# Flamingo block on one core: a re-ordered first stage, opening and border, and TensorE products on zeros

## What is computed

```
x += tanh(g0) * autocorrelation(layernorm(x), ctx, ctx)
x += tanh(g1) * mixture(layernorm(x))          # base product + 8 routed low-rank experts, top 2
x += tanh(g2) * attention(layernorm(x), ctx)   # 32 query heads, 8 key/value heads of 128, RMS norm
x += tanh(g3) * ffn(layernorm(x))              # W plus 8 low-rank updates
```

## Time and profile before

| | us |
|---|---|
| median of 3 runs | 821.94 (816.72 to 822.92) |
| the profiled execution | 821.45 |
| its span, first to last instruction | 819.7 |
| TensorE busy | 782.6 (95%) |
| VectorE busy | 559.7 (68%) |
| ScalarE busy | 415.0 (51%) |
| GpSimd busy | 365.5 (45%) |

### The profile page before, as it was taken

One profiled execution on the slowest core, in us unless ns is written; L12 is line 12 of the kernel. 1 busy time (PEld: TensorE's weight loads), 2 busy tenths in 40 slices (PEclk: granted clock), 3 DMA queues, 4 the chain that ended last, 5 costly groups with the idle time before them and its releaser, 6 DMA issues.

```text
span 819.7 us, 13174 instructions
## 1 busy us (share of the span) xinstructions
PE 782.6 (95%) x4224; PEld 634.8 (77%) x4224; DVE 559.7 (68%) x1235; ACT 415.0 (51%) x1158; POOL 365.5 (45%) x428
## 2 busy tenths in 40 slices
PE   4798889988999999999999999999999999999998
PEld 2354446567888888888888888888888888888776
DVE  4676667755777666777666777666777766777774
ACT  4355545355555644555554556544555554454421
POOL 2356665656333632453354336424632643254532
PEclk9899999998999999999999999999999999999999
DMA  8200001302100300030021002000300111000002
GB/s 302 93 27 27 26 27 34 109 1 90 28 14 1 104 26 1 1 104 27 1 61 57 14 1 91 29 12 1 103 27 1 34 46 52 2 14 1 1 27 77
DMA packets 17123, 34.61 MB, mean 42 GB/s; under 512 B 2336, under 2 KB 2592, under 8 KB 16800
## 3 DMA queue, kind: packets, MB, share of 16 engines
q1 hardware_dynamic: 17056, 33.78, 12.7%
HBM read 31.67 MB, written 2.10 MB: 41 GB/s over the span
## 4 chain that ended last, share of the span: by engine, by line
PE 74%; POOL 8%; DVE 7%; issue 6%; ACT 3%; DMA 1%; SPq 1%; POOLq 0%; ACTq 0%; DVEq 0%
PE pair L837 17%; PE pair L838 17%; PE pair L839 17%; PE pair L936 4%; PE pair L949 3%; PE pair L998 3%; PE pair L850 2%; POOL qkr L515 2%; POOL probn L507 2%; PE pair L938 1%; PE pair L874 1%; PE pair L891 1%; DMA bb<-in_bb 1%; POOL wo_lo L501 1%; PE pair L878 1%
## 5 line engine op out<-in xcount | busy, mean ns | idle before, releaser
L507 POOL TENSOR_TENSOR probn<-prob,erec 128x512 f32<-128x512 f32 x64 | 66.8, 1044 | 162.1 <-DVE erec L1315 162.1
L1320 DVE TENSOR_REDUCE qkss<-qksq 128x5 f32<-128x640 f32 x64 | 52.6, 821 | 90.3 <-ACT qksq L704 90.3
L1339 DVE TENSOR_TENSOR qkn<-pair,qkr 128x640 f32<-128x640 f32 x64 | 52.7, 824 | 89.5 <-POOL qkr L515 89.5
L697 ACT ACTIVATE prob<-score,nmax 128x128 f32<-128x128 f32 x256 | 99.6, 393 | 20.4 <-DVE nmax L1302 18.7
L837 PE MATMUL pair<-wq_hi,nT_hi 128*128 128x512 f32 x256 | 107.4, 420 | 0.0
L686 ACT ACTIVATE oT_hi<-pair 128x512 fp32r<-128x512 f32 x64 | 38.1, 595 | 136.2 <-PE pair L839 136.2
L837 PE MATMUL pair<-wo_hi,oT_hi 128*128 128x512 f32 x256 | 100.8, 394 | 2.8 <-issue 2.8
L839 PE MATMUL pair<-wq_hi,nT_lo 128*128 128x512 f32 x256 | 101.4, 396 | 0.0
L838 PE MATMUL pair<-wq_lo,nT_hi 128*128 128x512 f32 x256 | 101.4, 396 | 0.0
L838 PE MATMUL pair<-wo_lo,oT_hi 128*128 128x512 f32 x256 | 100.3, 392 | 0.0
L839 PE MATMUL pair<-wo_hi,oT_lo 128*128 128x512 f32 x256 | 99.7, 389 | 0.0
(11 more groups left out here) (173 smaller groups left out, 1990.3 us busy)
## 6 DMA issues: line engine op xcount, KB each, us to landing
wq_raw<-in_wq SPq DMA_DIRECT2D x32, 256.0 KB, 3.0
wo_raw<-in_wo SPq DMA_DIRECT2D x32, 256.0 KB, 2.9
wkv_raw<-in_wkv SPq DMA_DIRECT2D x8, 512.0 KB, 4.8
ctxn<-in_ctx_n SPq DMA_DIRECT2D x8, 256.0 KB, 3.1
ctxt<-in_ctx_t SPq DMA_DIRECT2D x8, 256.0 KB, 2.7
out<-wkv_raw SPq DMA_DIRECT2D x8, 256.0 KB, 2.0
xres<-in_x SPq DMA_DIRECT2D x1, 1280.0 KB, 11.0
wbase<-in_wbase SPq DMA_DIRECT2D x1, 1024.0 KB, 8.2
```

Of the source, the lines that this page charges most:

```text
L507: pool.tensor_tensor(probn[:], prob[:], erec[:].unsqueeze(2).broadcast_to([P, HG, P]), ALU.mult).then_inc(normed, 1)
L697: t = act.activation(prob[:, h, :], score[:, h, :], ACT.Exp, bias=nmax[:, h:h + 1], accum_out=esum[:, h:h + 1])
L1320: dve.tensor_reduce(qkss[:], qksq[:], AX.X, ALU.add).then_inc(qk_ss, 1)
L1339: dve.tensor_tensor(qkn[:], qk_bank, qkr[:].unsqueeze(2).broadcast_to([P, HG + 1, P]), ALU.mult).then_inc(qk_nat, 1)
```

## The change

The same instructions run in another order on all engines, with these additions: TensorE multiplies a 128x128 block of zeros (prod1, written by GpSimd as its first instruction) by itself ten times (`WARM`) while the first transfers run, and the identity by itself eight times after `q_transform(1)`; their results are not read. `q_transform(1)` writes the bank base_bank in place of corr_bank. The identity copy and the gating of bb move behind the first pick (`constants`); SP loads context 2 ahead of x of batches 3 to 7, and context 3 ahead of the turned context 1. In a slot, the low parts of weights and turned context precede `lag_weights` on GpSimd, and `low_rows` follows `h_scale`; on ScalarE `high_rows` goes from the end of a slot to the start of the next, and `high_turned_ctx` and `lag_exponents` are done for batch b+1 at the end of slot b. On TensorE `turn_out` goes ahead of the third context transform. At the border, `base_products` of batches 6 and 7 are split in halves, and the last steps of batch 7 go into slots 1 and 2. n1T and spare change places in SBUF.

The diff, with one line of context:

```diff
@@ -95,3 +95,3 @@
     kfb = early("kfb", [P, 4, D])
-    rest8, rest9, spare, wlag = (early(n, [P, CH, P]) for n in ("rest8", "rest9", "spare", "wlag"))
+    rest8, rest9, n1T, wlag = (early(n, [P, CH, P]) for n in ("rest8", "rest9", "n1T", "wlag"))
     op = [early(f"op{i}", [P, D]) for i in range(4)]
@@ -102,3 +102,3 @@
     ctxn = early("ctxn", [P, 2, D])
-    n1, n1T = early("n1", [P, D]), early("n1T", [P, CH, P])
+    n1, spare = early("n1", [P, D]), early("spare", [P, D])
 wo_raw = sb("wo_raw", [P, HG, D])
@@ -195,2 +195,5 @@
 
+def q_spectrum(b):
+    return base_bank if b == 1 else corr_bank
+
 def n2_bank(b):
@@ -215,2 +218,3 @@
 consts = sem("a_consts")
+zeros = sem("a_zeros")
 tanhed = sem("a_gates_tanh")
@@ -318,2 +322,3 @@
 PICK = 4
+WARM = 10
 ROUTE = 6
@@ -381,5 +386,6 @@
         sp.dma_start(bcat[:], bcat_d[:]).then_inc(ld_w[2], 16)
+        load_ctx(2)
         load_batches(2)
+        load_ctx(3)
         load_turned_ctx(1)
-        load_ctx(2)
         sp.dma_start(wkv_raw[:], wkv_d[0]).then_inc(ld_wkv, 16)
@@ -391,4 +397,5 @@
         for b in range(3, B):
+            if b > 3:
+                load_ctx(b)
             load_turned_ctx(b - 1)
-            load_ctx(b)
         load_turned_ctx(B - 1)
@@ -426,2 +433,3 @@
     def _(pool):
+        pool.memset(prod1[:, 0:P], 0.0).then_inc(zeros, 1)
         pool.memset(neghalf[:], -0.5).then_inc(consts, 1)
@@ -465,2 +473,4 @@
         def add_bias(b):
+            if b == 0:
+                pool.wait_ge(bias_gated, 1)
             pool.wait_ge(h_norm, b + 1)
@@ -500,2 +510,3 @@
                 pool.wait_ge(w_norm, B)
+                pool.wait_ge(h_out, B)
             pool.tensor_tensor(wo_lo[:, h, :], wo_raw[:, h, :], wo_hi[:, h, :].bitcast(F32),
@@ -517,5 +528,2 @@
         def a_slot(b):
-            low_turned_ctx(b)
-            if has(b - 3):
-                low_rows(b - 3)
             if b == 3:
@@ -525,3 +533,8 @@
                     low_wq(0, c)
+            if b > 0:
+                low_turned_ctx(b)
             lag_weights(b)
+            if b == 0:
+                f_scale(2)
+                low_turned_ctx(0)
             if has(b - 2):
@@ -530,2 +543,4 @@
                 h_scale(b - 1)
+            if has(b - 3):
+                low_rows(b - 3)
             if has(b - 2):
@@ -533,3 +548,3 @@
             sums(b)
-            if has(b + 2):
+            if b > 0 and has(b + 2):
                 f_scale(b + 2)
@@ -560,4 +575,8 @@
                 norm_probs(n)
+            if n == 1:
+                g_scale(B - 1)
             if on(n + 2):
                 inverse_norms(n + 2)
+            if n == 2:
+                low_rows(B - 1)
             if on(n) and n % B == 1:
@@ -573,3 +592,2 @@
         f_scale(1)
-        pool.wait_ge(bias_gated, 1)
         for b in range(B - 1):
@@ -594,6 +612,4 @@
 
-        g_scale(7)
         norm_probs(0)
         inverse_norms(2)
-        low_rows(7)
         low_wkv(1)
@@ -722,12 +738,10 @@
         def a_slot(b):
+            if has(b - 3):
+                high_rows(b - 3)
             if has(b - 2):
                 copy_hw(b - 2)
-            if b >= 1:
+            if b >= 2:
                 act.wait_ge(q_fwd, b + 1)
                 normalise(nx[:], b + 1, f_sc, f_root, f_norm)
-            high_turned_ctx(b)
-            lag_exponents(b)
             if b == 0:
-                copy_spectrum(1)
-                copy_swapped(1)
                 copy_quarter(1, 0)
@@ -751,6 +765,13 @@
                 copy_swapped(b + 2)
+            if b == 0:
+                high_turned_ctx(0)
+                normalise(nx[:], 2, f_sc, f_root, f_norm)
+            if b > 0:
+                high_turned_ctx(b + 1)
+            lag_exponents(b + 1)
+            if b == 0:
+                high_turned_ctx(1)
+            if has(b + 2):
                 copy_quarter(b + 2, 0)
                 copy_quarter(b + 2, 1)
-            if has(b - 2):
-                high_rows(b - 2)
 
@@ -765,2 +786,4 @@
                 high_qk(n + 1)
+            if n == 2:
+                high_rows(B - 1)
             if n == CLOSING:
@@ -781,2 +804,4 @@
                 high_v(n + 2)
+            if n == 1:
+                normalise(n2[:], B - 1, g_sc, g_root, g_norm)
             if on(n) and b == 1:
@@ -790,8 +815,11 @@
         copy_swapped(0)
-        act.wait_ge(ld_g, 16)
-        act.activation(gate[:], gates_in[:], ACT.Tanh).then_inc(tanhed, 1)
         copy_quarter(0, 0)
+        copy_quarter(0, 1)
         act.wait_ge(q_fwd, 1)
         normalise(nx[:], 1, f_sc, f_root, f_norm)
-        copy_quarter(0, 1)
+        act.wait_ge(ld_g, 16)
+        act.activation(gate[:], gates_in[:], ACT.Tanh).then_inc(tanhed, 1)
+        copy_spectrum(1)
+        lag_exponents(0)
+        copy_swapped(1)
         for b in range(B - 1):
@@ -799,5 +827,4 @@
 
+        high_rows(4)
         copy_hw(5)
-        high_turned_ctx(7)
-        lag_exponents(7)
         copy_lags(7)
@@ -819,12 +846,10 @@
         high_v(1)
-        route_exponents(7)
         high_rows(6)
+        route_exponents(7)
 
-        copy_hw(7)
         high_qk(1)
         exponents(0)
-        normalise(n2[:], 7, g_sc, g_root, g_norm)
+        copy_hw(7)
         squares(2)
         high_v(2)
-        high_rows(7)
         high_wkv(1)
@@ -842,4 +867,5 @@
             pe.wait_ge(f_norm, b + 1)
-            need(pe, picked, PICK * b - 1)
-            pe.matmul(corr_bank, dft[:, K_FWD, :], nx[:], start=True, stop=True).then_inc(q_fwd, 1)
+            if b >= 2:
+                pe.wait_ge(picked, PICK * b - 1)
+            pe.matmul(q_spectrum(b), dft[:, K_FWD, :], nx[:], start=True, stop=True).then_inc(q_fwd, 1)
 
@@ -854,2 +880,4 @@
             pe.wait_ge(c_prod, 2 * b + 2)
+            if b == 1:
+                pe.wait_ge(picked, PICK * b - 1)
             for j in range(CH):
@@ -1071,6 +1099,4 @@
                 base_products(b - 2)
-            if b == 0:
-                ctx_transform(1, 1)
-                ctx_transform(1, 2)
-            q_transform(b + 1)
+            if b > 0:
+                q_transform(b + 1)
             turn_lags(b)
@@ -1078,2 +1104,4 @@
                 routed_product(b - 2)
+            if b < 2:
+                ctx_transform(b + 2, 0)
             lag_transforms(b)
@@ -1085,3 +1113,3 @@
                 project_kv(0)
-            if has(b + 2):
+            if b >= 2 and has(b + 2):
                 ctx_transform(b + 2, 0)
@@ -1093,3 +1121,2 @@
                 ctx_transform(b + 2, 1)
-                ctx_transform(b + 2, 2)
             if b == B - 2:
@@ -1098,2 +1125,4 @@
                 turn_out(b - 2)
+            if has(b + 2):
+                ctx_transform(b + 2, 2)
 
@@ -1105,2 +1134,7 @@
                 turn_probs(n - 1)
+            if n == 1:
+                base_products(B - 1, (2, 3))
+                routed_product(B - 1)
+            if n == 2:
+                turn_out(B - 1)
             if chunk(n, FOLD) is not None:
@@ -1124,2 +1158,5 @@
 
+        pe.wait_ge(zeros, 1)
+        for i in range(WARM):
+            pe.matmul(h_bank[:, 0:P], prod1[:, 0:P], prod1[:, 0:P], start=True, stop=True)
         pe.wait_ge(ld_dft[0], 16)
@@ -1129,5 +1166,10 @@
         pe.wait_ge(ld_dft[1], 16)
-        correlation(0)
         ctx_transform(0, 2)
+        correlation(0)
         ctx_transform(1, 0)
+        ctx_transform(1, 1)
+        q_transform(1)
+        for i in range(8):
+            pe.matmul(h_bank[:, 0:P], dft[:, IDENT, :], dft[:, IDENT, :], start=True, stop=True)
+        ctx_transform(1, 2)
         for b in range(B - 1):
@@ -1145,7 +1187,8 @@
         router(6)
+        base_products(6, (0, 1))
         turn_out(5)
+        base_products(6, (2, 3))
 
-        base_products(6)
-        inverse(7)
         turn_hw(6)
+        inverse(7)
         routed_product(6)
@@ -1158,9 +1201,8 @@
 
-        base_products(7)
+        base_products(7, (0, 1))
         scores(0)
-        turn_hw(7)
         turn_qk(1)
-        routed_product(7)
-        project_qkv(2)
-        turn_out(7)
+        project_q(2, range(CH))
+        turn_hw(7)
+        project_kv(2).then_inc(qkv_done, 1)
         slots(slot)
@@ -1198,3 +1240,3 @@
                 dve.wait_ge(k_copied, 5 * b + 3)
-            dve.tensor_tensor((prod1, prod2)[i][:], corr_bank, kfa[:, i, :], ALU.mult).then_inc(c_prod, 1)
+            dve.tensor_tensor((prod1, prod2)[i][:], q_spectrum(b), kfa[:, i, :], ALU.mult).then_inc(c_prod, 1)
 
@@ -1364,8 +1406,20 @@
 
+        def constants():
+            dve.wait_ge(ld_dft[1], 16)
+            dve.tensor_copy(ident[:], dft[:, IDENT, :]).then_inc(ident_done, 1)
+            dve.wait_ge(tanhed, 1)
+            dve.wait_ge(ld_w[3], 16)
+            dve.tensor_scalar(bb[:], bb[:], gate[:, 1:2], None, ALU.mult).then_inc(bias_gated, 1)
+
         def a_slot(b):
             pick_lags(b)
+            if b == 0:
+                corr_product(1, 0)
+                corr_product(1, 1)
+                constants()
```

(67 more changed lines are left out.)

## The result

The changed kernel takes 791.47 us (4 runs, 791.35 to 791.68) against 819.33 us (4 runs, 815.46 to 822.92): 27.9 us less, ratio 0.9661, 95% interval 0.9607 to 0.9715. The prediction was 792.3 us, in 787 to 801. The profiled execution has a span of 789.6 us against 819.7: 30.1 us less.

What follows compares the result with a forecast made beforehand. TensorE bounds the last 629 us; the 190.5 us before them hold waits and half clock. Opening 10.8, slots 14.2 and border 4.2 sum to 29.2 us, taken from 821.45: 792.3 us, range 787 to 801.

Steps and rivals of the forecast that it cites:

- opening, to base(0): From the start to batch 0's base product on TensorE: earlier picks and kept clock gain 10.8 us, bounds 7 and 11.5.
- five slots: First stage, slots 2 to 6: waits and half clock go, 14.2 us gained, bounds 7.5 and 15.5.
- border and after: Between first stage and attention: TensorE's waits filled by reordered work, net 4.2 us, bounds 2 and 5.3.
- The pause of 1.0 us ahead of inverse(0): Opening: TensorE's one pause found, waiting for GpSimd's sums; the clock might fall in it.
- The doubt about the load of x: Opening: x for batches 3 to 7, issued later, lands at 18, needed at 19.6; at 11.0 us again, 1.6 us late.
- three chains within 0.3 us of each other: Slots: VectorE, nx and TensorE nearly tie, which costs something: 15.65 us a slot instead of TensorE's 15.4.
- Rival 1: Slots stay partly long, 17.0 us or more with some half clock: 7 us less gain, about 800; chance 0.17.
- rival 2: Slots: GpSimd and VectorE shut each other out, the pick grows by up to 1.26 us: 796; chance 0.08.
- rivals 4 and 5: 4: waits only move to ScalarE's queue, 814, chance 0.03. 5: lower clock in the long stretch, 827, chance 0.03.
- one mechanism: Slots: GpSimd's low parts first and ScalarE's exponents one batch early together remove the wait, slots 3 to 5 from 20.1 to 15.65.
- the move of low_rows: Slots: low_rows goes behind h_scale on GpSimd; the moves cost their engines nothing new.
- a sign of being wrong: Stated test: wrong if slots stay above 18 us or the long last stretch (629 us) changes its length.

Runs made afterwards that it cites:

- Run 6: Changed kernel with the identity copy and gating of bb ahead of the first pick on VectorE, as before: 793.95 us, 2.5 more.
- run 7: Changed kernel without the ten products on zeros: 791.47 us, the same median.
- run 2: Changed kernel with ScalarE's cast of the turned context and exponents back in their own batch's slot, batches 2 to 7: 796.68 us, 5.2 more.
- run 1: Changed kernel with GpSimd's slot order as before (cT_lo, low_rows, low parts of the weights, then wlagn): 802.04 us, 10.6 more.
- run 5: Changed kernel with the border's order as before on every engine: 795.09 us, 3.6 more.
- run 10: Changed kernel with g_scale(7) behind inverse_norms(3), n2(7) behind high_wo, turn_out(7) after project_q(4), high_rows(7) behind slot 2's exponents: 790.16 us.
- run 4: Kernel before with only ScalarE's cast of the turned context and exponents done one batch early: 810.97 us, ratio 0.9892, 8.6 us less.
- run 8: Changed kernel without the eight identity products after q_transform(1): 791.63 us, 790.12 to 794.77 in four runs.
- run 12: Changed kernel without the ten products on zeros and without the eight identity products: 791.72 us (790.84 to 793.87).
- run 9: Changed kernel with eight identity products in TensorE's two waits of slot 2, five before turn_out(7), three before turn_qk(3): 789.86 us.
- run 11: Changed kernel with g_scale(7), n2(7), high_rows(7) later, turn_out(7) after project_q(4), eight identity products before turn_qk(3): 789.27 us, ratio 0.9633.

## Why the prediction was right

| step | forecast, us | in the traces |
|---|---|---|
| opening, to base(0) | 10.8 | 10.68 |
| five slots | 14.2 | 15.20 |
| border and after | 4.2 | 4.22 |
| sum | 29.2 | 30.1 |

The forecast started from a trace of the kernel before at a mean clock of 0.983, which is why the traces differ by more (30.1 us) than the medians (27.9).

**Opening.** The two picks were forecast at 12.6 and 23.9 and came at 12.25 and 23.74; from wlag(1) to base(0) it took 13.2 us where I had 12.8. The pause of 1.0 us ahead of inverse(0) was 1.12 and did not drop the clock; two shorter ones, 0.62 us before turn_lags(0) and 0.78 us before router(0), I had not named. Run 6 shows the wait for bb at 2.5 us by its median and 2.7 by its pick (forecast 2.3), and run 7 the first product at half clock at 1.07 (1.0). The doubt about the load of x was needless: it landed in 8.3 us.

**Slots.** The mechanism was right, the size slightly off: I gave 15.65 us a slot and 15.3 to the last for three chains within 0.3 us of each other, and they cost nothing; the slots are TensorE's 15.49 and 14.93. Rival 1 is out. So is rival 2: a replacement beside cT_lo takes its 0.28 us. So are rivals 4 and 5, by the slots and by the clock of 1.00 over the last 630 us. The Trainium skill, "SBUF — State Buffer", section "SBUF: two separate sides", has VectorE and GpSimd shut each other out only for VectorE instructions with two SBUF inputs or in a 2-port mode. The replacement reads one tile of 128x128 (its eight values are loaded by an instruction of their own), so these two rows agree with it; they don't show what two inputs would do.

What the prediction told as one mechanism is two, and they overlap. Undone in the changed kernel, GpSimd's order costs 10.6 us and ScalarE's 5.2; alone in the kernel before they give 12.5 and 8.6. GpSimd's takes TensorE's wait for wlagn away and leaves a slot of 16.45 us, with TensorE busy for 16.23 of it and VectorE still held up 2.23 us by the exponents; ScalarE's alone leaves 2.12 to 2.14 us of that wait, and in the changed kernel it takes the slot from 16.75 (run 2) to 15.49 us. With high_rows behind the exponents, low_rows ahead of wlagn would wait for it: 3.05 us in run 1, with the parts of wq queued behind. The prediction called the move of low_rows free, which it is; it did not say that leaving it would cost most of the slots' gain. Run 1 puts cT_lo back ahead of the weights too, so that low_rows is the costly one of the two is read off its trace, not tested alone.

**Border.** 4.22 us by the traces and 3.6 by run 5, against 4.2, and it is made up as forecast: 5.1 us less up to the scores of n = 2 (5.3 forecast), 0.9 us more behind them, turn_qk(3) coming later by as much, for g_scale(7) ahead of inverse_norms(3) (1.1 forecast; run 10, without it, gets 0.9 us back). So the long stretch did change its length, by 0.87 us, which I had listed as a sign of being wrong while my own sum had 1.1 us of it. The fall of the clock behind this wait was in the kernel before too, and stays.

**Clock.** Forecast as falling after every wait of some 2 us. Here it fell behind 2.57 and 2.50 us and not behind 2.17 (run 1), behind one of three waits of 2.12 to 2.14 us (run 4), behind pauses of 2.04 and 0.62 us in run 8 and not in run 12: after some pauses and not after others of the same length. The Trainium skill, "TensorE: Matmul & The Clock Gate", Part 1, says of the rise of the clock that its moment varies from run to run; these runs show as much of the fall.

## What to carry to other kernels

Before moving work, find which engine's queue holds the late instruction, and which instruction ahead of it is itself waiting: here one reorder of GpSimd gave 12.5 us, and with it done VectorE's wait for ScalarE's exponents was the next thing to take away. Stop at the point where TensorE is busy for the whole slot at full clock (15.49 of 15.49 us); beyond it only its work counts. A pause of 2 us on TensorE costs the pause, and in some runs about 1.7 us more (0.17 of ten microseconds at the border); products on anything at hand in a pause that has no work of its own took that away at the border and moved the rows behind by no more than 0.03 us (run 9).

## What was not expected of the hardware

The spread of a kernel's runs goes with its mean granted clock, and so, as far as runs 8, 9 and 11 show, with its pauses. The kernel before has 814.9 us at a mean granted clock of 0.992 and 822.6 at 0.981 with the same program; the changed kernel stays within 0.33 us at 0.997 to 0.998, that of run 11, with its one long wait at the border filled, within 0.26 us, and taking the identity products out widened it to 4.65 us (790.12 at 1.000, 794.77 at 0.994). Products of zeros by zeros raised the clock: 2.04 us for the first product without them (runs 7 and 12), 1.10 with them in seven of nine traces, and 1.69 and 1.49 in those of runs 5 and 10. The clock column does not show this: the earlier trace rows has 1.00 from 0 to 16 us, where the first product takes the 2.04 us of the lower level. So a run that starts at half clock can have a mean of 1.000, as two of run 7 had at 791.90 and 792.05 us. Where TensorE waited for the first context, it landed at anything from 5.35 to 6.83 us, and everything behind it shifts by that, so a gain of 1 us in the opening is not told from it in four runs. In runs 1, 6 and 11 the products of zeros took 4.19 to 4.44 us and the first product followed with no wait, so they may have held it up a little there.
